# Experts stage of a vision tower: second products split into a rounded part and its rest, elementwise work dealt anew to three engines

## The reference, cut to what matters

```python
def _L0_ffn_ref(x, w_fc_sh, w_proj_sh, w1, w2, router_w, balance_bias):
    shared = _mlp(x, w_fc_sh, w_proj_sh)         # square(relu(x @ wfc)) @ wproj
    scores = sigmoid(xf @ router_w.T)            # 8 experts
    _, idx = top_k(scores + balance_bias, 2)
    tw = take(scores, idx); tw = tw / (tw.sum(-1) + 1e-20)
    combine = (one_hot(idx, E) * tw[..., None]).sum(1)
    h = square(relu(einsum('nc,ech->neh', xf, w1)))
    y = einsum('neh,ehc->nec', h, w2)
    return shared + einsum('nec,ne->nc', y, combine)
h = h + _L0_ffn_ref(_layernorm(h), ...)
```

## Time and profile before

| | us |
|---|---|
| median of 3 runs | 4549.45 |
| lowest, highest | 4533.93, 4564.05 |
| the profiled execution's own time | 4544.49 |
| its span | 4542.5 |

### The profile page before, as it was taken

How to read it: one execution, slowest core, us unless ns; L and a number is a source line. 1 busy time by engine, 2 the same in 40 slices (tenths; PEclk the granted TensorE clock), 3 DMA queues, 4 the chain that set the end, 5 groups by cost and what they waited for, 6 DMA issues and landing times. The chain is left out here.

```text
span 4542.5 us, 84795 instructions
## 1 busy us (share of the span) xinstructions
PE 4128.4 (91%) x28203; PEld 4011.3 (88%) x28203; DVE 2946.3 (65%) x7462; ACT 2474.0 (54%) x6670; POOL 1266.1 (28%) x1418
## 2 busy tenths in 40 slices
PE   4984799899899999989989999998999699999999
PEld 4984599899899989989989998998998599999999
DVE  4674466666666656666666666666666477777777
ACT  2552666556666656656655665666664244444443
POOL 1233122222222222213212222222222144444443
PEclk8997899999999999999999999999999799999999
DMA  8542000000000000000000000000000122222222
GB/s 181 134 108 66 2 1 1 1 23 1 1 23 1 1 2 23 1 1 23 1 1 11 13 1 2 23 1 1 12 1 1 45 85 87 92 96 94 87 87 84
DMA packets 88737, 161.69 MB, mean 36 GB/s; under 512 B 5579, under 2 KB 75810, under 8 KB 84704
## 3 DMA queue, kind: packets, MB, share of 16 engines
q1 hardware_dynamic: 84896, 152.66, 11.9%
q0 software_dynamic: 944, 2.42, 0.3%
q10 hardware_dynamic: 2560, 2.36, 0.2%
HBM read 127.82 MB, written 29.60 MB: 35 GB/s over the span
## 5 line engine op out<-in xcount | busy, mean ns | idle before, releaser
L602 POOL TENSOR_TENSOR att_prob<-att_prob,att_total 99x396 f32<-99x396 f32 x768 | 650.7, 847 | 2353.0 <-DVE att_total L848 2353.0
L678 ACT ACTIVATE att_probT<-att_t 99x396 f32<-99x396 f32 x768 | 385.1, 501 | 1044.3 <-PE att_t L994 1041.1
L856 DVE TENSOR_REDUCE att_npeak<-att_s 99x2 f32<-99x396 f32 x768 | 436.7, 569 | 746.6 <-PE att_s L1028 742.9
L1011 PE MATMUL att_o<-att_probT,att_vx 99*96 99x198 f32 (+1 forms) x3072 | 675.4, 343 | 27.8 <-DVE att_rx L841 26.8
L1028 PE MATMUL att_s<-att_kx,att_qx 96*99 96x198 f32 (+1 forms) x3072 | 664.6, 339 | 6.1 <-issue 5.7
L690 ACT ACTIVATE att_prob<-att_s,att_npeak 99x198 f32<-99x198 f32 x1536 | 636.7, 424 | 17.5 <-DVE att_npeak L856 17.0
L1195 POOL TENSOR_TENSOR ffn_hidden<-ffn_relu 128x384 f32<-128x384 f32 x462 | 417.7, 909 | 510.9 <-ACT ffn_relu L1224 508.6
L1011 PEld LDWEIGHTS att_o<-att_probT,att_vx 99*96 99x96 f32 (+1 forms) x3072 | 505.0, 182 | 58.6 <-issue 38.0
L1028 PEld LDWEIGHTS att_s<-att_kx,att_qx 96*99 96x99 f32 (+1 forms) x3072 | 522.7, 170 | 23.5 <-issue 7.0
L1224 ACT ACTIVATE ffn_relu<-ffn_h 128x384 f32<-128x384 f32 x462 | 226.1, 490 | 496.7 <-PE ffn_h L1433 495.8
L1445 PE MATMUL ffn_y<-ffn_down,ffn_hidden 128*128 128x192 f32 x2772 | 487.1, 326 | 0.0
(11 more groups left out here) (204 smaller groups left out, 8126.8 us busy)
## 6 DMA issues: line engine op xcount, KB each, us to landing
ffn_gates<-gate_rows SPq DMA_DIRECT2D x66, 768.0 KB, 5.1
tok_pixels<-in_x SPq DMA_DIRECT2D x24, 1568.0 KB
ffn_hid<-hidden SPq DMA_DIRECT2D x35, 288.0 KB, 3.0
att_xres<-hidden SPq DMA_DIRECT2D x8, 1188.0 KB
hidden<-att_xres SPq DMA_DIRECT2D x8, 1188.0 KB
...
```

The lines of the kernel that those rows point to most:

```text
L602: nc.gpsimd.tensor_tensor(prob[:, i % 2, :, :], prob[:, i % 2, :, :], view(total[:, i % 2, :], [[1, 2], [0, NTOK]]), ALU.mult).then_inc(pr ...
L678: nc.scalar.activation(probT[:, i % 2, :], t_bank[0:HALF, 0:2 * NTOK], ACT.Copy).then_inc(probT_made, 1)
L856: nc.vector.tensor_reduce(npeak[:, i % 2, :], s_bank[i % 2][0:HALF, 0:2 * NTOK].rearrange("p (h k) -> p h k", h=2), AX.X, ALU.max, negate= ...
L1011: ins = nc.tensor.matmul(o_bank[0:M, 0:NTOK], vx[:, 2 * b + k, p % 2, v0:v0 + M], probT[:, j % 2, k * NTOK:(k + 1) * NTOK], start=(k == 0) ...
```

## The change

The diff touches `experts_stage` alone.

- The second weights are kept as an fp32r high part and an fp32r rest side by side (`down[:, j, 0]` and `down[:, j, 1]`), made once: ACT copies `raw_down`, DVE subtracts. `hidden` is split chunk by chunk in the same way into `hh` (ACT copy, `split_high`) and `hl` (POOL subtract, `rest`), seven slots each.
- A down tile is two fp32r matmuls in place of one float32 matmul: `hh` times both parts (384 columns), and `hl` times the high part (192 columns). `sums` adds two halves of each bank, six adds in place of three.
- Squares: of even n on ACT (`Square` from the relu buffer), of odd n on DVE (max of the PSUM bank and 0, times the relu buffer). The bank of an odd chunk is thus free only when DVE has done its square; `up` waits for `squared[1]` there.
- Gates: on POOL (`gate_chunk`), one multiply a chunk, since `gates` now holds a plane for each of the 12 chunks. They are loaded in eight DMAs in place of two, and 12 planes in place of 8.
- ACT works a chunk as relu (n), `split_high` (n + 2), square (n); POOL as `gate_chunk` (n + 3), `rest` (n + 2). For n = 1 the relu comes ahead of the copy of the logits and the exp. In the prologue DVE's route of block 0 stands between the squares of chunks 7 and 8.

```diff
-        down = m.sb("down", [128, HT, DIM])
+        raw_down = m.sb("raw_down", [128, HT, DIM])
+        down = m.sb("down", [128, HT, 2, DIM], fp32r)
+        hh, hl = m.sb("hh", [128, SPLITS, BT], fp32r), m.sb("hl", [128, SPLITS, BT], fp32r)
         hidden = m.sb("hidden", [128, 2, HT, BT])
-        relu = m.sb("relu", [128, 4, BT])
+        relu = m.sb("relu", [128, 2, 2, BT])
+        relu_made = m.sem("relu_made")
         odds = m.sb("odds", [128, BT])
         gateT = m.sb("gateT", [EXPERTS, BT])
-        gates = m.sb("gates", [128, 2, EXPERTS, BT])
+        gates = m.sb("gates", [128, 2, HT - 2, BT])
...
                     for h in range(2):
-                        half = EXPERTS // 2
-                        src = gate_rows[s, half * h:half * (h + 1), :]
-                        sp.dma_start(gates[:, s, half * h:half * (h + 1), :],
-                                     bass.AP(tensor=src.tensor, offset=src.offset, ap=[[0, 128], [BT, half], [1, BT]])
-                                     ).then_inc(gates_in[s][h], 16)
+                        for c, lo, hi, first in ((0, 0, 128, 0), (2, 0, 128, 1), (1, 0, 64, 0), (1, 64, 128, 1)):
+                            src = gate_rows[s, 4 * h + first, :]
+                            sp.dma_start(view(gates[lo:hi, s, 6 * h + c, :], [[3 * BT, 2], [1, BT]]),
+                                         bass.AP(tensor=src.tensor, offset=src.offset, ap=[[0, hi - lo], [2 * BT, 2], [1, BT]])
+                                         ).then_inc(gates_in[s][h], 16)
...
-                def squares(k, s):
-                    for n, j in enumerate(CHUNKS):
-                        rows = 64 if j == 13 else 128
-                        pool.wait_ge(relu_made, k * HT + n + 1)
-                        nc.gpsimd.tensor_tensor(hidden[0:rows, s, j, :], relu[0:rows, (n + 2 * s) % 4, :], relu[0:rows, (n + 2 * s) % 4, :], ALU.mult
-                                                ).then_inc(squared, 1)
-
-                squares(0, 0)
+                def gate_chunk(k, pair, s, n):
+
+                    if n in (SHARED, SHARED + GATED // 2):
+                        pool.wait_ge(gates_in[s][0 if n == SHARED else 1], pair * 64 + 64)
+                    pool.wait_ge(squared[n % 2], k * (HT // 2) + n // 2 + 1)
+                    j = CHUNKS[n]
+                    nc.gpsimd.tensor_tensor(hidden[:, s, j, :], hidden[:, s, j, :], gates[:, s, j, :], ALU.mult).then_inc(gated, 1)
+
+                def rest(k, s, n):
+
+                    pool.wait_ge(hh_made, k * HT + n + 1)
+                    nc.gpsimd.tensor_tensor(hl[:, n % SPLITS, :], hidden[:, s, CHUNKS[n], :], hh[:, n % SPLITS, :].bitcast(fp32), ALU.subtract
+                                            ).then_inc(split_made, 1)
+
+                def block_of(k, pair, s, more):
+                    gate_chunk(k, pair, s, SHARED)
+                    for n in range(HT):
+                        if n + LEAD + 1 < HT:
+                            gate_chunk(k, pair, s, n + LEAD + 1)
+                        if n + LEAD < HT:
+                            rest(k, s, n + LEAD)
+                        elif more:
+                            rest(k + 1, 1 - s, n + LEAD - HT)
+
+                for n in range(LEAD):
+                    rest(0, 0, n)
                 with pool.Fori(0, (BLOCKS - 1) // 2) as pair:
                     for s in range(2):
-                        squares(pair * 2 + s + 1, 1 - s)
+                        block_of(pair * 2 + s, pair, s, True)
+                block_of(BLOCKS - 1, BLOCKS // 2, 0, False)
...
                 def relu_of(k, s, n):
+                    act.wait_ge(up_done, k * HT + n + 1)
                     rows = 64 if CHUNKS[n] == 13 else 128
-                    act.wait_ge(up_done, k * HT + n + 1)
                     if n >= 4 or not isinstance(k, int):
-                        act.wait_ge(squared, k * HT + n - 3)
+                        act.wait_ge(squared[n % 2], k * (HT // 2) + n // 2 - 1)
+                    nc.scalar.activation(relu[0:rows, n % 2, (n // 2 + s) % 2, :], h_bank[n % 2][0:rows, 0:BT], ACT.Relu).then_inc(relu_made, 1)
                     if CHUNKS[n] == 13:
                         if not isinstance(k, int):
                             act.wait_ge(routed, k)
-                        nc.scalar.activation(odds[0:EXPERTS, :], h_bank[n % 2][64:64 + EXPERTS, 0:BT], ACT.Copy)
-                    nc.scalar.activation(relu[0:rows, (n + 2 * s) % 4, :], h_bank[n % 2][0:rows, 0:BT], ACT.Relu).then_inc(relu_made, 1)
-                    if CHUNKS[n] == 13:
+                        nc.scalar.activation(odds[0:EXPERTS, :], h_bank[1][64:64 + EXPERTS, 0:BT], ACT.Copy).then_inc(odds_made, 1)
+                        act.wait_ge(odds_made, k + 1)
+                        nc.scalar.activation(odds[0:EXPERTS, :], odds[0:EXPERTS, :], ACT.Exp, scale=-1.0).then_inc(expo_made, 1)
+
+                def square(k, s, n):
+                    if n % 2 == 0:
                         act.wait_ge(relu_made, k * HT + n + 1)
-                        nc.scalar.activation(odds[0:EXPERTS, :], odds[0:EXPERTS, :], ACT.Exp, scale=-1.0).then_inc(expo_made, 1)
+                        nc.scalar.activation(hidden[:, s, CHUNKS[n], :], relu[:, 0, (n // 2 + s) % 2, :], ACT.Square).then_inc(squared[0], 1)
+
+                def split_high(k, s, n):
+
+                    if n < SHARED:
+                        act.wait_ge(squared[n % 2], k * (HT // 2) + n // 2 + 1)
+                    else:
+                        act.wait_ge(gated, k * GATED + n - SHARED + 1)
+                    if n == SPLITS - 1:
+                        act.wait_ge(down_done, k * TB)
+                    else:
+                        act.wait_ge(chunk_done, k * (HT - 1) + n + SPLITS + (0 if n >= SPLITS else 1))
+                    nc.scalar.activation(hh[:, n % SPLITS, :], hidden[:, s, CHUNKS[n], :], ACT.Copy).then_inc(hh_made, 1)
...
+                act.wait_ge(w_in, 16 * WEIGHTS)
+                nc.scalar.activation(down[:, :, 0, :], raw_down[:, :, :], ACT.Copy).then_inc(down_high, 1)
+                act.wait_ge(down_cleared, 2)
+                for n in range(LEAD):
+                    split_high(0, 0, n)
                 with act.Fori(0, (BLOCKS - 1) // 2) as pair:
                     for s in range(2):
                         it = pair * 2 + s
                         for n in range(HT):
                             relu_of(it + 1, 1 - s, n)
+                            if n + LEAD < HT:
+                                split_high(it, s, n + LEAD)
+                            else:
+                                split_high(it + 1, 1 - s, n + LEAD - HT)
+                            square(it + 1, 1 - s, n)
...
-                def gate_hidden(it, pair, s, n):
-
-                    j = CHUNKS[n]
-                    i, c = j // 3, j % 3
-                    if n == SHARED or n == SHARED + GATED // 2:
-                        h = 0 if n == SHARED else 1
-                        dve.wait_ge(gates_in[s][h], pair * 16 + 16)
-                    dve.wait_ge(squared, it * HT + n + 1)
-                    halves = {0: ((0, 128, 2 * i),), 1: ((0, 64, 2 * i), (64, 128, 2 * i + 1)), 2: ((0, 128, 2 * i + 1),)}[c]
-                    for lo, hi, e in halves:
-                        ins = nc.vector.tensor_tensor(hidden[lo:hi, s, j, :], hidden[lo:hi, s, j, :], gates[lo:hi, s, e, :], ALU.mult)
-                    ins.then_inc(gated, 1)
+                def square(k, s, n):
+
+                    if n % 2:
+                        j = CHUNKS[n]
+                        rows = 64 if j == 13 else 128
+                        dve.wait_ge(relu_made, k * HT + n + 1)
+                        nc.vector.scalar_tensor_tensor(hidden[0:rows, s, j, :], h_bank[1][0:rows, 0:BT], 0.0,
+                                                       relu[0:rows, 1, (n // 2 + s) % 2, :], ALU.max, ALU.mult).then_inc(squared[1], 1)
...
                         dve.wait_ge(down_done, it * TB + t + 1)
-                        nc.vector.tensor_tensor(acc[:, s, t, :], y_bank[t][:, 0:DIM], acc[:, s, t, :], ALU.add).then_inc(summed, 1)
+                        nc.vector.tensor_tensor(acc[:, s, t, :], y_bank[t][:, 0:DIM], acc[:, s, t, :], ALU.add).then_inc(half_summed, 1)
+                    for t in range(TB):
+                        dve.wait_ge(half_summed, it * TB + t + 1)
+                        nc.vector.tensor_tensor(acc[:, s, t, :], y_bank[t][:, DIM:2 * DIM], acc[:, s, t, :], ALU.add).then_inc(summed, 1)
...
-                route(0, first_steps, range(4))
+                for n in range(HT):
+                    if n == 8:
+                        route(0, first_steps, range(4))
+                    square(0, 0, n)
...
+                dve.wait_ge(down_high, 1)
+                nc.vector.tensor_tensor(down[:, :, 1, :], raw_down[:, :, :], down[:, :, 0, :].bitcast(fp32), ALU.subtract
+                                        ).then_inc(down_low, 1)
...
```

(25 more changed lines are left out.)

23 lines of the change are left out of this document (15 added, 8 removed).

## The result

| | before | after | forecast |
|---|---|---|---|
| median, us | 4545.62 (4 runs) | 4815.11 (4 runs) | 4690 |
| lowest, highest | 4533.93, 4564.05 | 4807.99, 4828.21 | 4545 to 4765 |
| span of the profiled execution | 4542.5 | 4826.4 | |
| a body of the loop | 27.41 | 35.06 | 31.4 |

The ratio is 1.0592 with an interval of 1.0547 to 1.0638: 5.9% slower. The direction was forecast; the size was not, and the time lies 50 us above the range.

A forecast was written before the change was run, and what follows sets the result against it. PE bound the kernel before; after the change it was to wait for DVE's squares behind the route, body 31.4 us. 4544.5 + 128 (32 bodies) + 6 (prologue) + 8 (tail) = 4686.5, said as 4690; range 4545 to 4765.

The forecast's parts named there:

- The down tile at 0.283: On PE, matmuls of 384 and 192 columns take 0.175 and 0.108 us, 0.283 a tile in place of 0.327.
- Up 5's end to up 11's start, 14.3 us: Mid-body chain of relu 5, squares, route parts and statistics takes 14.3 us against PE's 9.8, so PE waits 4.5.
- POOL's price: Each gate product or rest on POOL costs 0.877 us from start to start, 26 of them 22.8 us a body.
- The gates 1 us into the next body, covered by POOL's slack: At the body's head, the gates' first half lands about 1 us in; POOL's slack in the last three chunks covers it.
- The waits at the exp and the square root: PE waits 0.8 us a body for the exp; ACT's square root waits for statistics, its table loaded during the wait.
- PE's wait for DVE, 4.5 us a body: PE waits for DVE's squares, some 2.5 us before up 9 and 2 before up 11.
- The ends: Outside the loop: body 0 begins about 6 us later, and the tail after the last body grows by 8 us.
- the cheap route: Rival, chance 0.15: DVE's small instructions slip between POOL's, POOL sets the pace, body 26.5 us, median 4535.
- PE as the bound: Rival, chance 0.07: PE stays the bound with every square in time, body 25.6 us, median 4505.
- POOL slower still: Rival, chance 0.10: POOL's instructions at 1.15 us on the mean, some 33 us a body, 4740; the clock goes the same way.

The follow-up runs named there:

- The first experiment: The kernel before, with POOL multiplying relu by a constant tile of ones in place of relu by itself: 4550.36 us, body 27.63.
- The second: The changed kernel, with both POOL instructions (gate product and rest) reading one tensor twice: 4671.04 us, body 31.18.
- the last kernel with the weights split early: Changed kernel with squares on ACT, gate products on DVE, gates turned after up 9, eight gate planes, second weights split earlier in the prologue: 4580.73 us.
- With twelve planes: Changed kernel with squares on ACT, gate products on DVE, gates turned after up 9, twelve gate planes kept: 4578.28 us, body 28.40.

## Why the prediction was right in direction and wrong in size

The mechanism held in the middle of the body: PE waits for DVE's squares, the squares stand behind the route, and the route's small instructions are held by POOL's. Two steps failed: the price of POOL's instruction was too low, and the gates' arrival was put at nothing. By the marks each leaves 1.8 us a body. Step by step:

- **The down tile at 0.283.** Right: 0.28 by the starts at full clock. So the change's own gain, 1.8 us a body, is there, and is spent.
- **Up 5's end to up 11's start, 14.3 us.** In the body shown it runs from 4142.4 to 4157.34, 14.9 us. Relu 5 takes 1.5, as forecast; parts 1 and 2 6.8 for 6.2; part 3 2.6, as forecast; statistics, root, relu and square 2.9 for 2.8. From the logits to the rows the miss is 1.8. Beside these 0.6 it holds POOL's pace between ups 4 and 8, 3.89 us a pair for the 3.51 of the forecast, and the half clock; how they share the rest isn't separated.
- **POOL's price, the first step that failed.** The terms are 26 x 0.877 = 22.8 us and the route at block 0's price. Measured from start to start it is 0.97, so 25.2 us, and parts 1 and 2 take 6.8. "Two different operands cost the same an element" divided a whole duration by its elements. That hides what an instruction costs apart from them, and a short one pays most of that. A second row with two different tensors stands in the trace of before, and I had not used it (groups of POOL: busy us, mean ns | idle before; the first row is used further below):

```profile
L602 POOL TENSOR_TENSOR att_prob<-att_prob,att_total 99x396 f32<-99x396 f32 x768 | 650.7, 847 | 2353.0 <-DVE att_total L848 2353.0
...
L607 POOL TENSOR_TENSOR att_xres<-att_xres,att_pbias 99x192 f32<-99x192 f32 x128 | 75.7, 591 | 0.0
```

  With 5898 ns for 2688 elements the slope is (5898 - 591) / (2688 - 192) = 2.13 ns an element and the rest 0.18 us; 384 elements then cost 1.00 us, which is what came out (1.01). The first experiment shows that price in the kernel before. The second bounds what it was worth: 3.9 us a body for 0.184 us from start to start, of which the forecast had missed 0.092.
- **The gates 1 us into the next body, covered by POOL's slack: the second step that failed.** Wrong in size and in reach. They come 3.6 us in. Six broadcast reads more cost SP time too: its two issues took 0.83 us, the eight take 4.61. And I looked only at POOL's slack, not at what stands behind the first product on ACT: `split_high` 2, then relu 1. It was put at nothing and is worth up to 2.8 us a body, 2.6 of it at the border, as the kernel with the gates read once shows. Without it the border takes 9.1 us for the forecast's 9.9, so other terms there were too dear by 0.8.
- **The waits at the exp and the square root.** Right: PE waits for the exp 16.1 / 26 = 0.6 us a body (0.8), and ACT waits for the statistics with its table loaded. No table load is added by Square.
- **PE's wait for DVE, 4.5 us a body.** Measured 4.3, and this is no success: it was to be before up 9 and up 11, and is before up 3 and up 9. Two errors cancel in the total.
- **The ends.** Prologue +9.3 us for 6: PE waits 6.6 us for the rest of the second weights (below), and before that 2.8 us for square 9, ahead of up 11, where block 0's route stands. Tail +12.4 for 8: 24 POOL instructions 0.97 apart in place of 0.877 would be 2.2 of it.

```profile
3673.15 0.68 PE L1495 MATMUL ffn_h<-ffn_x0h,ffn_w0h 128*128 128x384 f32 x1 [6.61 <-DVE ffn_down L1426]
...
4807.72 1.00 POOL L1211 TENSOR_TENSOR ffn_hl<-ffn_hidden,ffn_hh 128x384 fp32r<-128x384 f32 x1
4808.68 1.00 POOL L1206 TENSOR_TENSOR ffn_hidden<-ffn_hidden,ffn_gates 128x384 f32<-128x384 f32 x1
```

By terms: the bodies miss by 244.5 - 128 = 116.5 us and the ends by 7.7; 124 of the 125 between 4690 and 4815.

Of the rivals, the cheap route falls with the 0.93 us of its instructions, and PE as the bound with its idle time. "POOL slower still" had the right engine and the clock, at 0.10 and for another reason (long DVE instructions beside it), and put the end too low, at 4740, because it let POOL be the bound all along. POOL sets the pace between ups 4 and 8; over the stretch it is busy for 72%, and it waits for the gates at the head of each body. The range failed because its upper end, a body of 33.5 from POOL's own time and late start, holds neither the DVE instructions that the price stretches nor the wait before up 3.

The Trainium skill (GPSIMD Engine Reference, 4.1 Engine selection) calls two-input elementwise work about two times slower there than on VectorE. Measured: 1.01 us against 0.558, 1.8 times; as a duration the forecast's estimate of 1.12 was nearer than its 0.83. The same page (8. Key points) names VectorE instructions with two SBUF inputs, or in a 2-port perf mode, as those that contend with GpSimd. For two SBUF inputs the trace agrees, 0.93 against 0.18 us, while the square from PSUM and SBUF stays at 0.56.

**What stays open.** Moving work off both DVE and POOL brought the body to 28.4, still 1.0 above before and 2.8 above PE's own work. PE's visible waits there are 1.9 us a body (653.1 us busy in a stretch of 700, 24.6 bodies, granted clock 1.00). Most of it stands before the transposes of the gates, in the last kernel with the weights split early (waits, 3800 to 4500 us):

```profile
PE ffn_r L1476 <- DVE ffn_gate L1376: 32.7, 25, 1.3
```

Turned one chunk earlier, the gates are no longer finished in time. With twelve planes this wait is missing and the body as long, so no run tells which round of waits sets the length. The share of the clock in the 3.9 us of POOL's price isn't separated either. No version here beats the kernel before.
